# Five stages of an eight-stage fp32 network: order of work in the prologues, one step's maxima, a rotary shuffle and one weight transfer

## The chip, the cores and the metric

The kernel runs on one core of one Trainium2 chip. Time is device microseconds from start to end of the program; the kernel before takes 2041.01 us (median of 3 runs, 2038.54 to 2042.52). Engines are named as in the profile: PE (matrix engine; PEld its weight loads), DVE (vector), ACT (scalar), POOL (GpSimd), SP (issues the DMAs). Each engine runs its own queue of instructions in order and waits on semaphores.

## What is computed

Four pairs of an attention block and a feed-forward block on x of 4 x 512 x 256 values, each with a layer norm ahead and a residual add. The changed stages are the four attentions and the first feed-forward block.

```python
x = x + _L0_attn_ref(_layernorm(x, axis=-1), ...)   # rotary, ALiBi, window mask, 16 heads of 16, 8 kv heads
x = x + _L0_ffn_ref(_layernorm(x, axis=-1), ...)    # silu(x @ Wg.T) * (x @ Wu.T), then @ Wd.T, 256 -> 1024 -> 256
x = x + _L1_attn_ref(_layernorm(x, axis=-1), ...)   # causal, 16 heads of 16
x = x + _L1_ffn_ref(x, ...)                         # spline table
x = x + _L2_attn_ref(_layernorm(x, axis=-1), ...)   # causal, rotary
x = x + _L2_ffn_ref(_layernorm(x, axis=-1), ...)    # 8 experts, top 2
x = x + _L3_attn_ref(_layernorm(x, axis=-1), ...)   # not causal, heads mixed between sequences
x = x + _L3_ffn_ref(_layernorm(x, axis=-1), ...)    # 8 experts, top 2
```

## The kernel before

build() runs the stages one after the other with a barrier of all engines between them. X stays in SBUF as 16 tiles of 128 tokens; a batch b (NB = 4) is 4 tiles, 512 tokens. All orders of work are written out by hand: each stage has one program per engine, and the attention loops take small pieces of the next batch's preparation at the steps that a table `plan` gives. In what follows n is the step within a batch (32 steps of a batch) and N the step over all batches (128).

**Stage a0, attention_window (10 to 407 us of the trace).** The prologue prepares batch 0: DVE normalises (L102), PE turns the tiles (L556) and projects them (L568), DVE multiplies by the rotary tables (rotate, L380 and L383), POOL adds the two products (rotated, L298), ACT rounds to the high part (L467) and POOL takes the low part (lower, L306). SP stores the parts and fetches them back in another layout (L240, L243, L256, L259); these fetches end before the first scores (L592). The masks' constant columns in p are written by POOL in two memsets (L317 and L319), and POOL adds the bias to X (add_bias, L293). Batch 1's statistics are taken in the prologue also; its 1/sqrt is made by POOL (layer_norm_pool, L114 and L116), DVE then applies it (L102) and sums it (total, L343). In the loop DVE takes minima of the scores (L361), ACT the exponentials (L492), PE turns and multiplies them.

**Stage f0, swiglu (407 to 573 us).** SP loads wi (2 MB, L1386) and wd (1 MB, L1387). Weights and inputs are split into a rounded high part (ACT, L1475 and L1478 for weights, L1455 for the input) and a low part (DVE, L1441, L1445 and L1417). PE makes three products for each of KC = 2 chunks of 128 rows (L1503 to L1505), starting with chunk 0. In its queue a wait for all three low weights stands ahead of the loop over batches.

**Stages a1, a2, a3, attention_quads (574 to 882, 996 to 1335, 1550 to 1887 us).** The prologue: layer norm (L102), PE turns (L1178), ACT rounds weights (L1133, L1135) and input (L1138), DVE takes the low parts (L1039, L1044), PE projects (L1189 to L1191). In the loop, each step N has in PE's queue: scores_T(N) (L1234 to L1243), the scores of two tiles 24 tiles ahead (L1214 to L1219), on odd steps values (L1257), then the piece of the plan. DVE takes two maxima (maxima, L987) and then its part of the piece; ACT takes the exponentials (L1160) and its part. The scores use two PSUM banks, so PE waits in scores for the maxima of two tiles back.

The maxima of a group of heads are put together once in 8 steps: POOL's split_maxima (L938, L947, L948) makes two columns of them, PE turns these at n = 6, 14, 22, 30 (turn_maxima, L1265), and ACT and DVE copy them into q (L1095 and L992). POOL runs split_maxima at N % 8 == 4, as the last thing of the step. Its other work in the loop without rotary (a1, a3) is split_kept (L930, L932: two operations) for each turned or projected unit; at n = 12 there is one. With rotary (a2) DVE's rotate (L1012, L1013) ends in a stream_shuffle (L1016) of the sine product, POOL adds the two products (rotated, L907), ACT rounds (upper, L1091) at n = 6, 9, 11, 14 (`raised`) and POOL takes the low part (L914). In a2 the projections stand at n = 4, 7, 9, 12.

Of the kernel before, what the change touches and what calls it, by code (L numbers as in the profile page):

```python
# [13 lines left out]
NB = 4  # L14
S = 512
# [103 lines left out]
def attention_window(nc, tag, X, cst, PS, scr, weights, rope, scale, dist, slopes, bias):  # L119
# [12 lines left out]
    with ExitStack() as ctx:  # L132
# [87 lines left out]
        with nc.Block() as block:  # L220
# [52 lines left out]
            def _(pool):  # L273
# [35 lines left out]
                layer_norm_pool(pool, ln, 0, neg_half)  # L309
                weigh(0)  # L310
                rotated(0, 0)
                lower(0, 0)
                rotated(0, 1)
# [3 lines left out]
                pool.memset(p[:, :, :, KW:S], 0.0).then_inc(tails_done, 1)  # L317
                pool.wait_ge(tails_done, 1)
                pool.memset(p[0:GLOB, :, 0, :], 1.0).then_inc(p_ready, 1)  # L319
                add_bias(0)  # L320
                layer_norm_pool(pool, ln, 1, neg_half)
# [372 lines left out]
def attention_quads(nc, tag, X, Y, cst, PS, scr, filled, weights, masks=None, rope=None, bias=None, scrambled=False):  # L694
# [15 lines left out]
    with ExitStack() as ctx:  # L710
# [59 lines left out]
        else:  # L770
# [4 lines left out]
            for i, n in enumerate((4, 7, 9, 12) if rope is not None else (8, 9, 10, 12)):  # L775
                plan[n] = ("project", 1, i)
        raised = {6: 0, 9: 1, 11: 2, 14: 3} if rope is not None else {}
# [58 lines left out]
        with nc.Block() as block:  # L836
# [56 lines left out]
            def _(pool):  # L893
# [66 lines left out]
                for N in range(FULL):  # L960
                    kind, b, i = piece_at(N)
                    if kind == "turn":
# [9 lines left out]
                    if N % 8 == 4 and N // 8 + 1 < NB * NG:  # L972
                        split_maxima(N // 8 + 1)

            @block.vector
            def _(dve):
# [30 lines left out]
                def rotate(b, u, bank):  # L1007
# [5 lines left out]
                    dve.tensor_tensor(comp[:, u % 2, 0, :], PS[:, bank, :], tabs[:, 0, :], ALU.mult).then_inc(cos_done, 1)  # L1013
                    dve.wait_ge(sin_done, NU * b + u + 1)
# [22 lines left out]
                for i, w in enumerate((wqk_in, wv_in)):  # L1037
# [3 lines left out]
                                      ALU.subtract).then_inc(w_low_done, 1)  # L1041
                for c in range(KC):
                    dve.wait_ge(split_x, c + 1)
                    dve.tensor_tensor(x_low[:, c, :], PS[:, c, :], xnT[:, c, :].bitcast(F32),  # L1044
                                      ALU.subtract).then_inc(x_done, 1)
                if rope is not None:
                    dve.wait_ge(loaded_tab, 16)
                    for u in range(NU):
                        rotate(0, u, (2 + u) % 4)
                else:  # L1050
# [12 lines left out]
                for N in range(FULL):  # L1063
# [3 lines left out]
                    piece(*piece_at(N))  # L1067
                    if N % STEPS == 24 and N // STEPS + 2 < NB:
# [8 lines left out]
            def _(act):  # L1077
# [56 lines left out]
                act.wait_ge(loaded_v, 16)  # L1134
                act.activation(w_high[1][:, :, :].rearrange("p a b -> p (a b)"), wv_in, ACT.Copy).then_inc(w_high_done, 1)  # L1135
                for c in range(KC):
                    act.wait_ge(transposed, c + 1)
                    act.activation(xnT[:, c, :], PS[:, c, :], ACT.Copy).then_inc(split_x, 1)  # L1138
# [214 lines left out]
def swiglu(nc, tag, X, cst, PS, w_in, w_down):  # L1353
# [7 lines left out]
    with ExitStack() as ctx:  # L1361
# [21 lines left out]
        with nc.Block() as block:  # L1383
# [100 lines left out]
            def _(pe):  # L1484
# [8 lines left out]
                def batch(b, ahead):  # L1493
# [13 lines left out]
                    if ahead:  # L1507
                        turn(b + 1)
# [1323 lines left out]
```

## Time and profile before

| | |
|---|---|
| median of 3 runs | 2041.01 us (2038.54 to 2042.52) |
| the profiled execution | 2034.73 us |
| its span, first to last instruction | 2032.8 us |
| PE busy | 1631.1 us, 80% |
| DVE busy | 1186.2 us, 58% |
| ACT busy | 977.1 us, 48% |
| POOL busy | 470.7 us, 23% |
| mean granted PE clock | 0.878 of full speed |

Read it as an average over eight stages, each with limits of its own. A stage begins with a chain of engines that hand one batch to each other, with PE idle most of the time; after that PE is busy nearly always. A clock of 0.5 in a stretch is the 1.2 GHz level, 1.0 the 2.4 GHz level.

### The profile page before, as it was taken

What the parts mean: (1) busy time and instruction counts of PE and PEld (TensorE: products, weight loads), DVE (VectorE), ACT (ScalarE), POOL (GpSimd) and SP (SyncE); (2) the same over time, 40 slices, a digit from 0 to 9 for tenths busy, and PEclk for the clock granted to TensorE, in tenths of its full rate; (3) what the DMA queues carried; (4) which work ended last, traced back from release to release, by engine and by line L of the source; (5) the groups of instructions that cost most, each with busy time, mean ns of one, the idle gap of its engine ahead of it and who ended that gap; (6) DMA issues with size and microseconds to landing.
All of it is one profiled execution on the core that took longest, in us unless ns stands there. A gap on an engine that the chain in (4) does not pass through costs nothing. (4 is left out here: it accounts for less than half of the span.)

```text
span 2032.8 us, 29515 instructions
## 1 busy us (share of the span) xinstructions
PE 1631.1 (80%) x10710; PEld 1004.2 (49%) x10710; DVE 1186.2 (58%) x2606; ACT 977.1 (48%) x1547; POOL 470.7 (23%) x546
## 2 busy tenths in 40 slices
PE   3899999869968999921268899959996799988676
PEld 2455555558855555511245555546775344433433
DVE  2576767442345664659756665545444677775375
ACT  1677879632314544523024444536663366566321
POOL 4220210022323322020222321015664323210100
PEclk8799999979977999965559888978998699899598
DMA  6242240010044345010155325031112355140322
GB/s 212 52 100 53 63 94 1 1 63 0 0 139 120 93 115 146 2 48 0 54 130 146 104 59 130 1 118 47 48 48 70 98 145 142 36 114 1 112 84 84
DMA packets 66900, 156.14 MB, mean 77 GB/s; under 512 B 9853, under 2 KB 15366, under 8 KB 65994
## 3 DMA queue, kind: packets, MB, share of 16 engines
q1 hardware_dynamic: 66762, 154.32, 27.1%
q8 instruction: 84, 1.38, 0.3%
q14 instruction: 54, 0.44, 0.1%
HBM read 104.86 MB, written 51.52 MB: 77 GB/s over the span
## 5 line engine op out<-in xcount | busy, mean ns | idle before, releaser
L987 DVE TENSOR_REDUCE a_mx<-PS 128x1 f32<-128x512 f32 (+3 forms) x768 | 396.0, 553 | 199.8 <-PE PS L1219 124.3
L1160 ACT ACTIVATE a_pT<-PS 128x1024 f32<-128x1024 f32 (+3 forms) x384 | 308.7, 811 | 241.4 <-PE PS L1243 174.6
L1214 PE MATMUL PS<-a_k,a_q 64*128 64x512 f32 (+3 forms) x768 | 251.4, 452 | 68.4 <-DVE a_mx L987 39.0
L361 DVE CUSTOM_DVE_ANT_0 PS<-PS,a_dist 128x448 f32<-128x448 f32 x256 | 155.0, 648 | 72.0 <-PE PS L592 71.0
L1234 PE MATMUL PS<-a_q,a_k 64*128 64x512 f32 (+3 forms) x768 | 180.9, 451 | 11.3 <-DVE a_q L992 6.1
L1214 PEld LDWEIGHTS PS<-a_k,a_q 64*128 64x128 f32 x768 | 117.0, 204 | 128.0 <-DVE a_mx L987 93.2
L1257 PE MATMUL PS<-a_pT,a_va 128*32 128x512 f32 (+3 forms) x1536 | 173.0, 524 | 6.0 <-ACT a_raw L1118 6.0
L492 ACT ACTIVATE a_p<-PS,a_negm 128x448 f32<-128x448 f32 (+1 forms) x256 | 149.2, 640 | 3.4 <-DVE a_negm L361 1.9
L602 PE MATMUL PS<-cst,a_p 128*128 128x128 f32 x1024 | 143.1, 282 | 4.4 <-ACT a_pT L500 1.9
L1234 PEld LDWEIGHTS PS<-a_q,a_k 64*128 64x128 f32 x768 | 80.2, 193 | 117.0 <-issue 90.7
L602 PEld LDWEIGHTS PS<-cst,a_p 128*128 128x128 f32 x1024 | 110.9, 142 | 38.2 <-issue 32.7
L500 ACT ACTIVATE a_pT<-PS 128x512 f32<-128x512 f32 x205 | 115.0, 604 | 28.2 <-PE PS L602 26.8
L1926 POOL TENSOR_TENSOR f_h_low<-f_prod,f_h_high 128x512 fp32r<-128x512 f32 x84 | 109.5, 1310 | 60.9 <-ACT f_h_high L2113 56.0
L1095 ACT ACTIVATE a_q<-PS 16x1024 fp32r<-16x1024 f32 x48 | 48.7, 1016 | 104.1 <-PE PS L1265 103.8
L2049 DVE TENSOR_TENSOR f_prod<-PS,f_gb 128x512 f32<-128x512 f32 x84 | 57.3, 687 | 68.0 <-ACT PS L2139 66.0
L1217 PE MATMUL PS<-a_half_masks 64*128 64x128 bf16 x512 | 92.5, 245 | 0.0
L592 PE MATMUL PS<-a_k,a_q 48*128 48x448 f32 x256 | 63.2, 490 | 26.5 <-ACT a_p L492 16.8
L2139 ACT ACTIVATE PS<-PS,f_b 128x512 f32<-128x512 f32 x84 | 55.5, 660 | 51.1 <-PE PS L2213 51.0
L938 POOL TENSOR_TENSOR a_mxh<-a_mx,a_m 128x16 fp32r<-128x16 f32 x48 | 10.9, 227 | 294.5 <-DVE a_mx L987 294.5
L1219 PE MATMUL PS<-a_half_masks 64*128 64x64 bf16 x512 | 76.3, 201 | 0.0
L592 PEld LDWEIGHTS PS<-a_k,a_q 48*128 48x128 f32 x256 | 25.2, 192 | 100.3 <-issue 57.1
L992 DVE TENSOR_SCALAR a_q<-PS 16x1024 fp32r<-16x1024 f32 x48 | 59.0, 1230 | 20.9 <-PE PS L1265 19.9
(342 smaller groups left out, 3433.3 us busy)
## 6 DMA issues: line engine op xcount, KB each, us to landing
spread_scratch<-a_high SPq DMA_DIRECT2D x96, 256.0 KB, 6.5
a_q<-spread_scratch SPq DMA_DIRECT2D x96, 256.0 KB, 5.8
a_k<-spread_scratch SPq DMA_DIRECT2D x96, 256.0 KB, 6.6
f_gb<-gate_rows SPq DMA_DIRECT2D x68, 256.0 KB, 5.3
spread_scratch<-a_low SPq DMA_DIRECT2D x48, 256.0 KB, 7.4
window_scratch<-a_high SPq DMA_DIRECT2D x24, 256.0 KB, 2.3
a_q<-window_scratch SPq DMA_DIRECT2D x32, 192.0 KB, 5.9
a_k<-window_scratch SPq DMA_DIRECT2D x32, 192.0 KB, 6.3
```

The lines of the kernel that those rows point to most:

```text
L361: dve.tensor_tensor_reduce(PS[:, bank, 0:KW], PS[:, bank, 0:KW], dt_[:, off:off + KW], float(slopes[2 * pair + a]), 3e38, ALU.add, ALU.min ...
L492: act.activation(p[p0:P, GH * (gg % 2) + i, qt, 0:KW], PS[p0:P, bank, 0:KW], ACT.Exp, bias=negm[p0:P, bank:bank + 1], scale=-1.0).then_inc ...
L500: act.activation(pT[:, J % 2, i, :], PS[:, 4 + e % 2, :], ACT.Copy).then_inc(turned_act, 1)
L592: pe.matmul(PS[:, 2 * (N % 2) + a, 0:KW], q[rows, slot, half, qt * P:(qt + 1) * P], k[rows, slot, half, GLOB:S], start=True, stop=True).th ...
L602: mm = pe.transpose(PS[:, 4 + e % 2, qt * P:(qt + 1) * P], p[:, GH * (gg % 2) + i, qt, kt * P:(kt + 1) * P], ident)
L987: dve.tensor_reduce(mx[:, gg % 2, qt, 2 * half + a:2 * half + a + 1], PS[:, 4 + a, 0:kw], AX.X, ALU.max).then_inc(max_done, 1)
L1160: act.activation(pT[:, N // 2 % 2, N % 2, :, q0:S], PS[:, 2 * (N % 2):2 * (N % 2) + 2, q0:S], ACT.Exp, scale=SCALE).then_inc(exp_done, 1)
L1214: mm = pe.matmul(ps[:, 0:kw], q[rows, b % 2, pair, qt * P:(qt + 1) * P], k[rows, b % 2, pair, 0:kw], start=True, stop=not causal)
L1217: pe.matmul(ps[:, kw - P:kw], half_masks[rows, 0, 0, :], half_masks[rows, 1, 0, :], start=False, stop=False)
L1234: mm = pe.matmul(PS[:, 2 * half + a, q0:S], k[rows, b % 2, pair, kt * P:(kt + 1) * P], q[rows, b % 2, pair, q0:S], start=True, stop=not ca ...
L1257: mm = pe.matmul(PS[BLK * i:BLK * i + BLK, 6, q0:S], va[:, b % 2, kt, GH * g + i, :], pT[:, J % 2, i // 2, i % 2, q0:S], start=(kt == 0), ...
L1926: pool.tensor_tensor(h_low[:, G % 6, :], prod[:, G % 6, :], h_high[:, G % 6, :].bitcast(F32), ALU.subtract).then_inc(h_low_done, 1)
```

## The change

In a0, POOL's two memsets of p move: the first behind the first 1/sqrt, the second behind lower(0, 0); the 1/sqrt of batch 1 goes ahead of the bias add of batch 0. In f0, wi comes in two transfers with a semaphore each, ACT and DVE split chunk 0 of the weights, then the input, then chunk 1, and PE waits for chunk 0 before its first product, for chunk 1 before the first product with it, and for the low part of wd ahead of the down projection. In the three quads stages ACT and DVE split the input ahead of the v weights, and split_maxima goes to the head of POOL's step. In a2 the shuffle becomes a function of its own (exchange), which in the loop runs one step after the products (`swaps`); in the prologue it follows them at once, as before.

```diff
@@ attention_window, POOL @@
                 layer_norm_pool(pool, ln, 0, neg_half)
+                pool.memset(p[:, :, :, KW:S], 0.0).then_inc(tails_done, 1)
                 weigh(0)
                 rotated(0, 0)
                 lower(0, 0)
+                pool.wait_ge(tails_done, 1)
+                pool.memset(p[0:GLOB, :, 0, :], 1.0).then_inc(p_ready, 1)
                 rotated(0, 1)
                 lower(0, 1)
                 rotated(0, 2)
                 lower(0, 2)
-                pool.memset(p[:, :, :, KW:S], 0.0).then_inc(tails_done, 1)
-                pool.wait_ge(tails_done, 1)
-                pool.memset(p[0:GLOB, :, 0, :], 1.0).then_inc(p_ready, 1)
+                layer_norm_pool(pool, ln, 1, neg_half)
                 add_bias(0)
-                layer_norm_pool(pool, ln, 1, neg_half)
                 add_bias(1)
@@ attention_quads @@
+        swaps = {5: 0, 8: 1, 10: 2, 13: 3} if rope is not None else {}
         raised = {6: 0, 9: 1, 11: 2, 14: 3} if rope is not None else {}
@@ POOL @@
                     kind, b, i = piece_at(N)
+                    if N % 8 == 4 and N // 8 + 1 < NB * NG:
+                        split_maxima(N // 8 + 1)
                     if kind == "turn":
...
-                    if N % 8 == 4 and N // 8 + 1 < NB * NG:
-                        split_maxima(N // 8 + 1)
@@ DVE @@
+                def exchange(b, u):
                     dve.wait_ge(sin_done, NU * b + u + 1)
                     dve.wait_ge(cos_done, NU * b + u + 1)
                     dve.stream_shuffle(comp[:, u % 2, 1, :], comp[:, u % 2, 1, :], swap).then_inc(swapped, 1)
...
-                for i, w in enumerate((wqk_in, wv_in)):
+                def weights_low(i, w):
...
+                weights_low(0, wqk_in)
                 for c in range(KC):
                     dve.wait_ge(split_x, c + 1)
...
+                weights_low(1, wv_in)
...
                         rotate(0, u, (2 + u) % 4)
+                        exchange(0, u)
...
                     piece(*piece_at(N))
+                    if N % STEPS in swaps and N // STEPS + 1 < NB:
+                        exchange(N // STEPS + 1, swaps[N % STEPS])
@@ ACT @@
-                act.wait_ge(loaded_v, 16)
-                act.activation(w_high[1][:, :, :].rearrange("p a b -> p (a b)"), wv_in, ACT.Copy).then_inc(w_high_done, 1)
                 for c in range(KC):
                     act.wait_ge(transposed, c + 1)
                     act.activation(xnT[:, c, :], PS[:, c, :], ACT.Copy).then_inc(split_x, 1)
+                act.wait_ge(loaded_v, 16)
+                act.activation(w_high[1][:, :, :].rearrange("p a b -> p (a b)"), wv_in, ACT.Copy).then_inc(w_high_done, 1)
@@ swiglu, SP @@
-                sp.dma_start(wi[:, :, :].rearrange("p a b -> p (a b)"), w_in[:, :]).then_inc(loaded_i, 16)
+                for c in range(KC):
+                    sp.dma_start(wi[:, c, :], w_in[:, c * 2 * HID0:(c + 1) * 2 * HID0]).then_inc(loaded_i[c], 16)
@@ DVE @@
+                weights_low(0)
                 input_low(0)
+                weights_low(1)
@@ ACT @@
+                weights_high(0)
                 input_high(0)
+                weights_high(1)
@@ PE @@
                             for c in range(KC):
+                                if n == 0 and part == 0:
+                                    pe.wait_ge(w_low_done, c + 1)
...
+                    pe.wait_ge(w_low_done, KC + 1)
                     for t in range(TB):
...
                 turn(0)
-                pe.wait_ge(w_low_done, KC + 1)
```

POOL's queue in the prologue of a0 (a_p is p, X<-X,a_bb the bias add, a_comp rotated, a_low lower), as one piece of the difference:

```order
 L116 TENSOR_TENSOR a_ln_rstd<-a_ln_vareps,a_neg_half 128x4
+L310 MEMSET a_p 128x32x64
 L284 TENSOR_SCALAR a_ln_xn<-a_ln_xn,a_cplx 128x256 x4
...
-L317 MEMSET a_p 128x32x64
-L319 MEMSET a_p 64x8x512
-L293 TENSOR_TENSOR X<-X,a_bb 128x256 x4
+L315 MEMSET a_p 64x8x512
...
+L114 TENSOR_TENSOR a_ln_vareps<-a_ln_meanvar,a_ln_eps 128x4
+L116 TENSOR_TENSOR a_ln_rstd<-a_ln_vareps,a_neg_half 128x4
+L293 TENSOR_TENSOR X<-X,a_bb 128x256 x8
```

The first memset now follows batch 0's 1/sqrt at once, with no wait ahead of it; the second 1/sqrt has neither memset nor bias add ahead of it, and all eight bias adds follow it.

DVE's queue in a2 at the projection of n = 12 of batch 2 (L987 is a maximum, L1012 and L1013 the two products, L1016 the shuffle, L992 the copy of the maxima). Before:

```order
L987 TENSOR_REDUCE a_mx<-PS 128x1 x2
L1012 TENSOR_TENSOR a_comp<-PS,a_tabs 128x512
L1013 TENSOR_TENSOR a_comp<-PS,a_tabs 128x512
L1016 STREAM_SHUFFLE a_comp<-a_comp 128x512
L987 TENSOR_REDUCE a_mx<-PS 128x1 x4
L992 TENSOR_SCALAR a_q<-PS 16x1024
```

And now:

```order
L988 TENSOR_REDUCE a_mx<-PS 128x1 x2
L1013 TENSOR_TENSOR a_comp<-PS,a_tabs 128x512
L1014 TENSOR_TENSOR a_comp<-PS,a_tabs 128x512
L988 TENSOR_REDUCE a_mx<-PS 128x1 x2
L1020 STREAM_SHUFFLE a_comp<-a_comp 128x512
L988 TENSOR_REDUCE a_mx<-PS 128x1 x2
L993 TENSOR_SCALAR a_q<-PS 16x1024
```

Two maxima, those of the next step, pass the shuffle.

## Rows read from the trace of the kernel before

**Rows 1.** Timeline of a0: start us, duration us, engine, line, operation [idle before <-releaser].

```profile
44.94 0.74 PE L592 MATMUL PS<-a_k,a_q 48*128 48x448 f32 x2 [9.38 <-DMA a_k<-window_scratch]
49.11 1.38 DVE L102 TENSOR_SCALAR a_ln_xn<-X,a_ln_meanvar,a_ln_rstd 128x256 f32<-128x256 f32 x4 [11.04 <-POOL a_ln_rstd L116]
50.64 1.09 PE L556 MATMUL PS<-cst,a_ln_xn 128*128 128x128 f32 x4 [4.96 <-DVE a_ln_xn L102]
53.58 1.21 ACT L492 ACTIVATE a_p<-PS,a_negm 64x448 f32<-64x448 f32 x2 [1.11 <-DVE a_negm L361]
54.81 0.60 ACT L455 ACTIVATE a_xT<-PS 128x512 f32<-128x512 f32 x1
55.55 3.75 PE L568 MATMUL PS<-a_xT,a_wqk 128*128 128x512 f32 x4
```

**Rows 2.** Timeline: the norm alone (a0), beside POOL (f0), beside a memset (f3).

```profile
13.79 1.38 DVE L102 TENSOR_SCALAR a_ln_xn<-X,a_ln_meanvar,a_ln_rstd 128x256 f32<-128x256 f32 x4 [1.50 <-POOL a_ln_rstd L116]
...
439.66 2.37 DVE L102 TENSOR_SCALAR f_ln_xn<-X,f_ln_meanvar,f_ln_rstd 128x256 f32 x4
...
1890.26 1.81 POOL L2363 MEMSET f_wts<- 128x2048 f32 x1
1890.35 2.83 DVE L102 TENSOR_SCALAR f_ln_xn<-Y,f_ln_meanvar,f_ln_rstd 128x256 f32<-128x256 f32 x4 [1.48 <-POOL f_ln_rstd L116]
```

**Rows 3.** DMA issues of f0: engine, KB each, us from issue to landing.

```profile
f_wi<-in_f_in SPq DMA_DIRECT2D x1, 2048.0 KB, 7.6
f_wd<-in_f_down SPq DMA_DIRECT2D x1, 1024.0 KB, 9.7
```

**Rows 4.** Timeline of f0, prologue (L1503 at 426.46 is the first of chunk 1).

```profile
414.87 3.71 ACT L1475 ACTIVATE f_wi_high<-f_wi 128x2048 fp32r<-128x2048 f32 x2 [16.00 <-DMA f_wi<-in_f_in]
416.81 4.50 DVE L1441 TENSOR_TENSOR f_wi_low<-f_wi,f_wi_high 128x2048 fp32r<-128x2048 f32 x2 [4.86 <-ACT f_wi_high L1475]
421.23 1.28 DVE L1417 TENSOR_TENSOR f_x_low<-PS,f_x_high 128x512 fp32r<-128x512 f32 x2
425.05 0.76 PE L1503 MATMUL PS<-f_x_high,f_wi_high 128*128 128x512 f32 x1 [11.06 <-DVE f_wd_low L1445]
426.46 0.63 PE L1503 MATMUL PS<-f_x_high,f_wi_high 128*128 128x512 f32 x1
```

**Rows 5.** Waits of PE in a1 (590 to 900 us): total us, times, longest.

```profile
PE PS L1265 <- POOL a_m L948: 4.3, 3, 1.4
```

**Rows 6.** Waits of PE in a3 (1550 to 1886 us).

```profile
PE PS L1265 <- POOL a_m L948: 4.5, 3, 1.6
```

**Rows 7.** Timeline of a1 and a3 at n = 12 to 14 of batch 0.

```profile
654.24 1.23 DVE L992 TENSOR_SCALAR a_q<-PS 16x1024 fp32r<-16x1024 f32 x1 [1.48 <-PE PS L1265]
...
1636.37 1.23 DVE L992 TENSOR_SCALAR a_q<-PS 16x1024 fp32r<-16x1024 f32 x1 [1.17 <-PE PS L1265]
```

**Rows 8.** Timeline of a2, prologue.

```profile
1002.94 0.63 ACT L1135 ACTIVATE a_w_highv<-a_pT 128x512 fp32r<-128x512 f32 x1 [0.98 <-DMA a_pT<-in_a_w]
1004.21 1.28 DVE L1044 TENSOR_TENSOR a_x_low<-PS,a_xnT 128x512 fp32r<-128x512 f32 x2
```

**Rows 9.** Waits of PE in the loop of a2 (1060 to 1238 us).

```profile
PE PS L1214 <- DVE a_mx L987: 13.6, 16, 1.4
PE PS L1265 <- POOL a_m L948: 2.3, 6, 0.4
```

**Rows 10.** Timeline of a2 from n = 4 to 9 of batch 0.

```profile
1061.71 0.73 DVE L1016 STREAM_SHUFFLE a_comp<-a_comp 128x512 f32<-128x512 f32 x1
1074.32 0.63 ACT L1091 ACTIVATE a_high<-a_comp 128x512 fp32r<-128x512 f32 x1 [0.95 <-POOL a_comp L907]
```

**Rows 11.** Windows in a1 and a2: us, PE, PEld, DVE, ACT, POOL busy, PEclk, DMA, GB/s.

```profile
716.61:733.72 17.11, 16.35 (x161) 10.10 (x161) 9.45 (x19) 7.94 (x12) 0.63 (x3) 1.00 0.82 224
782.63:802.14 19.51, 18.87 (x161) 11.61 (x161) 9.37 (x19) 8.00 (x12) 0.63 (x3) 0.83 0.88 227
1055.00:1245.00 190.00, 168.41 (x1518) 101.17 (x1519) 120.32 (x262) 83.02 (x123) 52.19 (x69) 0.88 0.39 106
```

More of the change, by code:

```diff
@@ L1374, in swiglu @@
         h_high, h_low = sb("h_high", [P, NHT, S], R32), sb("h_low", [P, NHT, S], R32)
-        loaded_i, loaded_d, preset = sem("loaded_i"), sem("loaded_d"), sem("preset")
+        loaded_i = [sem(f"loaded_i{c}") for c in range(KC)]
+        loaded_d, preset = sem("loaded_d"), sem("preset")
         w_high_done, w_low_done = sem("w_high_done"), sem("w_low_done")
@@ L1438, in _, with weights_low @@
                 layer_norm_dve(dve, ln, 0, lambda t: X[:, t, :])
-                for c in range(KC):
+                def weights_low(c):
                     dve.wait_ge(w_high_done, c + 1)
@@ L1471, in batch, with weights_high @@
                         input_high(b + 1)
-                act.wait_ge(loaded_i, 16)
-                for c in range(KC):
+                def weights_high(c):
+                    act.wait_ge(loaded_i[c], 16)
                     act.activation(wi_high[:, c, :], wi[:, c, :], ACT.Copy).then_inc(w_high_done, 1)
+                weights_high(0)
                 input_high(0)
+                weights_high(1)
                 act.wait_ge(loaded_d, 16)
```

## The prediction

> **What bounds the kernel now.** The page's busy shares come first: PE 80%, DVE 58%, ACT 48%, POOL 23%. PE bounds the sum, so a change pays where it ends idle time of PE or raises PE's clock (mean 0.878). The timeline of each prologue comes next, since PE idles there for long, then the waits of PE within each loop, and at last windows with the clock beside them. The reader is to see in each who comes last.
>
> In a0 PE's first scores wait for the DMA that brings the keys back and start at 44.94 [rows 1]. Batch 1 is not ready then: DVE has stood for 11.04 us, since 38.07, for POOL's 1/sqrt, and normalises only at 49.11; PE turns the tiles at 50.64, projects at 55.55 [rows 1]. In f0 PE's first product waits for the low part of wd, the last thing DVE does, and starts at 425.05 [rows 4]. In a1 and a3 PE stands for POOL's maxima, 4.3 and 4.5 us, three times each [rows 5, 6]. In a2 PE waits for DVE's maxima, 13.6 us in 16 waits, 0.85 each [rows 9].
>
> **a0.** Without the memsets and the bias add ahead of it, POOL makes batch 1's 1/sqrt soon after its last lower, some 3 us after DVE's statistics (38.07), near 41. DVE's norm takes 1.38 and is done before the scores start at 44.94, so the fetches bound the chain. From there, with the row's durations: the scores' 0.74 to 45.7, PE's turn 1.09, ACT's copy 0.60, the first exponential 1.21, the second copy 0.60, and about 0.1 between each: the projection starts at 49.6 instead of 55.55, a gain of 5.95 [rows 1]. If the chain from turn to projection kept its present length (50.64 to 55.55) behind a turn at 45.75, it would be 4.9.
>
> What it costs: the first memset now runs right behind batch 0's 1/sqrt, at the time DVE normalises batch 0, which is on the chain that ends in the fetches. Alone this norm takes 1.38; beside a memset of the same size in f3 it takes 2.83 [rows 2]. So +1.45 on everything behind. The bias add may now run beside batch 1's norm: beside one POOL operation it took 2.37, 1.0 more [rows 2]; but the scores still start later than that norm ends, so I take 0.3 (0 to 1.0). The second memset fits into POOL's idle time between the units of the prologue. Net 5.95 − 1.45 − 0.3 = **−4.2** (−2.5 to −6.0).
>
> The Trainium skill, "SBUF — State Buffer", section "Who interferes with whom", says of DVE in a two-port mode and GpSimd that "Whoever issues first gets the shared pair for the whole instruction; the other fully blocks". By that the norm waits for the whole memset, 1.8 instead of 1.45; the row of f3 shows the collision and 1.45, some less than the rule, so the trace agrees in kind.
>
> **f0.** wi lands 7.6 after its issue (at 414.8), wd 9.7 (417.3) [rows 3]: the second MB takes about 2.5 longer per MB, so the first half of wi should land at 412.3. ACT's copy of a chunk is 3.71/2 = 1.87, DVE's low part 4.50/2 = 2.25, the input's low part 1.28 [rows 4]. ACT has chunk 0 at 414.3; DVE is at it until 416.6 and has the input at 417.9; PE starts at 418.0 instead of 425.05. DVE's chunk 1 is done at 420.2, and PE's first product with it starts at 420.3 instead of 426.46: **−6.1**. The clock's rise moves with it. wd's low part follows 2.3 later, long before the down projection. If both halves land together at 414.8, each step is 2.3 later: −3.8.
>
> **a1, a3.** split_maxima goes ahead of split_kept in POOL's queue at n = 12. PE's turn then has its operand in time, and the next to be late would be DVE: in a1 it stood 1.48 behind that turn, in a3 1.17 [rows 7], so it gives nearly the whole wait back. split_kept comes some 0.7 later, for a projection a step away. **−4.2** and **−3.0**. ACT's and DVE's turned order in the prologue: the v weights are there before the input in a1 (0); in a3 −0.3 (0 to −0.6).
>
> **a2.** In the prologue ACT waits 0.98 for the v weights, and only then DVE takes x's low part, for which PE waits [rows 8]; now the input goes first: **−1.0**. In the loop DVE's shuffle, 0.73 [rows 10], no longer stands between the products and the next step's two maxima. The same shuffle then stands after the next step's maxima, where DVE has waits of its own (it does 120 us of work in 190 [rows 11]). PE's waits for the maxima and for POOL's turns are 13.6 + 2.3 = 15.9 [rows 9]; that is the upper bound. Against it: the two products alone take 1.4 and remain, and the parts come later: POOL adds the products after the shuffle, and ACT, which already waits 0.95 for that sum at n = 9 [rows 10], would wait some 2.3 longer, with the next exponentials behind it. I take 0.6 of 15.9, **−9.5** (−4 to −15.9).
>
> **Clock.** Equal work (161 matmuls) in a1 takes 17.11 at 1.00 and 19.51 at 0.83, 2.40 more [rows 11]. At half speed for 0.34 of 19.51 the records lose the equivalent of 3.3 full-speed us, so each costs 0.73. The loop of a2 stands at 0.88 for 190 us [rows 11]: 22.8 such us, worth 16.6. With fewer waits of PE part of it returns; I take a fifth, **−3** (0 to −15). That is my least certain term.
>
> The Trainium skill, "TensorE: Matmul & The Clock Gate", section "Terms", puts the penalty at the throttled time × (1 − K/N), which would make the dip of a1 3.3 and a2's 22.8; the trace has 2.40 for the first, so the sum goes by 0.73.
>
> **The sum.** 4.2 + 6.1 + 4.2 + 3.3 + 1.0 + 9.5 = 28.3, and 3 of clock: 31.3. The profiled execution took 2034.73 (span 2032.8), so 2003.4 for one like it. The median of the runs is 2041.01, 6.3 above that execution: 2009.7, or **2010**.
>
> **Rivals.**
> - *The clock returns in full.* If PE without gaps keeps the full clock in most of a2's loop and the dips of a1 and a3 go, the clock's term is −18 instead of −3: 1995. For it: the dip in a1 [rows 11]. Against: a2's 0.88 is a mean over 190 us, and PE still waits for ACT and DVE.
> - *The loops pay little.* Another engine takes each wait over: in a2 ACT at its wait for the sum, in a1 and a3 DVE at the copy of the maxima. Then the prologues' 11.6 remain, and some 2 to 3: 2027. For it: DVE is the busier one in a2, the maxima at a projection keep 1.4 of products ahead of them.
> - *Slower.* In a2 the shuffle a step later makes the sum 2.2 to 2.6 later; ACT's queue is in order, so at each of 12 projections the exponentials behind its copy are late, and PE stands for them. It decides if ACT has under 1 us of slack at each; at 2.6 × 12 = 31 lost, with a2's 9.5 and the clock's 3 not gained, the sum is 31 − 18.8: +12, 2053. Against: ACT is busy 83 of 190 us and PE waits for an exponential nearly nowhere.
> - *The change doesn't do what it says*: the memset holds DVE longer in a0, both halves of wi land together, and the waits in the loops remain with another name: 2038.
>
> **How the numbers follow.** Forecast 0.60, full clock 0.13, loops pay little 0.18, slower 0.04, no effect 0.05. The forecast's own bounds are a2 at −4, no clock and wi together (8 more, with a0 at its low end 10 more: 2020) and a2's 15.9 with some more clock (10 less: 2000). The range reaches on to the first two rivals, 1995 to 2027, and leaves out the last two and half of the first, with what lies beyond either end. A measurement of this kernel can tell 0.2%, 4.1 us, from no change: faster 0.91 (the first three cases), same 0.05, slower 0.04.
>
> **What the profile of the changed kernel would show.** Right: in a0 the norm of batch 0 at about 2.8 and no 11 us wait ahead of batch 1's, scores at about 46.4, the projection near 51.3. In f0 wi in two rows, the first landing about 5 after its issue and PE's first product 11 after it (18 before). In a1 and a3 no wait of PE for POOL at the turn. In a2 the waits for DVE's maxima at half or less, longer waits of ACT for POOL's sum. Wrong: these waits gone and PE waiting for ACT in their place; a norm of batch 0 at 1.4 (my cost is not there) or over 3; a clock in a2 that stays at 0.88 or reaches 0.95.

## Result and profile after

The changed kernel takes 1986.79 us (median of 4 runs, 1979.97 to 1990.48) against 2040.71 before: ratio 0.9732, 95% interval 0.9704 to 0.9761, or 54 us less. Timed once more on another chip it took 1985.39 against 2034.42: ratio 0.9767, 0.9738 to 0.9796, 49 us less. The profiled execution took 1990.48, its span is 1988.6, 44.2 less than the span of before.

From one stage's first norm to the next one's, in us, by the two traces:

| | a0 | f0 | a1 + f1 | a2 | f2 | a3 | f3 |
|---|---|---|---|---|---|---|---|
| before | 396.8 | 166.6 | 422.3 | 340.0 | 213.6 | 337.3 | 142.5 |
| changed | 392.7 | 160.6 | 414.9 | 320.0 | 214.4 | 329.2 | 142.9 |
| difference | −4.1 | −6.1 | −7.4 | −20.0 | +0.8 | −8.1 | +0.4 |

The two stages that the change doesn't touch stay within 0.8. a0 and f0 paid what the prediction gave them; the three stages with the quads loop paid far more.

The page, engines' busy time and the granted clock in 40 slices:

```profile
PE 1618.9 (81%) x10710; PEld 999.2 (50%) x10710; DVE 1183.9 (60%) x2606; ACT 977.4 (49%) x1547; POOL 472.3 (24%) x546
PEclk9899999979977999965569999869998799999598
```

PE executes the same 10710 instructions as before, yet its busy time is 12 us less: its instructions ran faster.

Timeline of a0 (start us, duration us, engine, line), the answer to [rows 1, 2]:

```profile
13.85 1.80 POOL L310 MEMSET a_p<- 128x2048 f32 x1
13.93 2.83 DVE L102 TENSOR_SCALAR a_ln_xn<-X,a_ln_meanvar,a_ln_rstd 128x256 f32<-128x256 f32 x4 [1.50 <-POOL a_ln_rstd L116]
L102 DVE TENSOR_SCALAR a_ln_xn<-X,a_ln_meanvar,a_ln_rstd x4: 394/401/1864, 13.9 to 16.4; 128x256 f32<-128x256 f32 x4
42.12 2.92 DVE L102 TENSOR_SCALAR a_ln_xn<-X,a_ln_meanvar,a_ln_rstd 128x256 f32<-128x256 f32 x4 [3.01 <-POOL a_ln_rstd L116]
46.01 0.74 PE L592 MATMUL PS<-a_k,a_q 48*128 48x448 f32 x2 [9.41 <-DMA a_k<-window_scratch]
50.43 3.75 PE L568 MATMUL PS<-a_xT,a_wqk 128*128 128x512 f32 x4
```

The norm of batch 0 takes 2.83 beside the memset, the figure taken from f3. The third line has the shortest, the median and the longest of its four instructions in ns: one is held and takes 1.86 us, until 15.79, just behind the memset's end at 15.65; the others take 0.40 as without a memset. The wait of 11.04 is 3.01, the scores start 1.07 later than before, the projection of batch 1 5.12 earlier.

DMA issues and timeline of f0's prologue, the answer to [rows 3, 4] (the stage's first norm stands at 406.67 here, at 410.58 before):

```profile
f_wi<-in_f_in SPq DMA_DIRECT2D x2, 1024.0 KB, 6.0
```

```profile
408.33 1.91 ACT L1492 ACTIVATE f_wi_high<-f_wi 128x2048 fp32r<-128x2048 f32 x1 [15.50 <-DMA f_wi<-in_f_in]
410.28 2.29 DVE L1455 TENSOR_TENSOR f_wi_low<-f_wi,f_wi_high 128x2048 fp32r<-128x2048 f32 x1 [2.22 <-ACT f_wi_high L1492]
413.87 0.76 PE L1525 MATMUL PS<-f_x_high,f_wi_high 128*128 128x512 f32 x1 [3.79 <-DVE f_x_low L1430]
416.02 0.79 PE L1525 MATMUL PS<-f_x_high,f_wi_high 128*128 128x512 f32 x1 [0.53 <-DVE f_wi_low L1455]
```

ACT starts 1.66 after the norm's start instead of 4.29, so the first half of wi is there 2.6 earlier, against the norm's start, than the whole was. PE's first product stands at +7.2 instead of +14.5, the first with chunk 1 at +9.35 instead of +15.88: 6.5 earlier.

Waits of PE (total us, times, longest) in a1 (580 to 883 us), then in a2's loop (1041 to 1206), then in a3 (1553 to 1841), the answer to [rows 5, 6, 9]; of each the first line:

```profile
PE PS L1225 <- DVE a_mx L988: 8.3, 15, 0.9
...
PE PS L1225 <- DVE a_mx L988: 5.2, 10, 0.6
...
PE PS L1225 <- DVE a_mx L988: 10.6, 18, 1.1
```

No wait for POOL at the turn (it would be L1276) is left anywhere, and none took its place: in a1 the wait for maxima is 8.3 where it was 8.4 before. In a2 the 15.9 of [rows 9] are 5.2. Behind the first scores, to the stage's end, the same two waits are 18.1 before (15.8 and 2.3) and 7.4 now: 10.7 less either way.

Windows of a2's loop (us, PE, PEld, DVE, ACT, POOL busy, PEclk, DMA, GB/s), the answer to the last of [rows 11]:

```profile
1041.00:1211.00 170.00, 157.39 (x1552) 96.59 (x1553) 121.54 (x270) 84.18 (x125) 49.07 (x66) 0.98 0.44 119
```

1552 matmuls in 170 us, where 1518 took 190, and the clock is 0.98 instead of 0.88. The two places in this loop where it still falls to the 1.2 GHz level, at 1106 and 1174, stand right behind its two longest waits, 1.65 us each for POOL's low part of x (L1200, at 1104.7 and 1173.0); none stands behind a wait for maxima, of which the longest is 0.6:

```profile
1104.00:1112.00 8.00, 7.29 (x62) 4.31 (x62) 5.38 (x10) 2.12 (x4) 2.42 (x5) 0.79 0.01 2
```

ACT's timeline in a2 shows what the late shuffle costs:

```profile
1053.70 0.63 ACT L1102 ACTIVATE a_high<-a_comp 128x512 fp32r<-128x512 f32 x1 [1.52 <-POOL a_comp L908]
```

ACT waits 1.52 where it waited 0.95 [rows 10], 8.3 instead of 5.2 in 190 us of the loop, and PE waits for no exponential behind it.

### The profile page after: what moved, and what is told of

Its sections match the earlier page's. It is cut to its first block and busy times, and to the rows that moved or that the text cites. A ratio compares the mean times of both kernels' runs of the same rounds, so it can differ in the third digit from the quotient of the medians.

```text
span 1988.6 us, 29520 instructions
## 1 busy us (share of the span) xinstructions
PE 1618.9 (81%) x10710; PEld 999.2 (50%) x10710; DVE 1183.9 (60%) x2606; ACT 977.4 (49%) x1547; POOL 472.3 (24%) x546
## 3 DMA queue, kind: packets, MB, share of 16 engines
q8 instruction: 84, 1.38, 0.3%
## 5 line engine op out<-in xcount | busy, mean ns | idle before, releaser
L616 PE MATMUL PS<-a_pT,a_va 128*32 128x512 f32 x512 | 68.8, 611 | 0.0
```

## Experiments

What was open: which part brought how much, and whether the excess over the prediction is the clock, a part that was priced too low, or a difference between runs. Runs of one kernel differ by up to 25 us on one chip (the kernel before: 2022.77 to 2047.90 in 27 runs, with the clock from 0.869 to 0.885), so each run is read by its ratio and by its stages. The ratios come from different chips, and each has its interval.

| | median | before, same chip | ratio (95%) | a0 | f0 | a1 + f1 | a2 | a3 | f3 |
|---|---|---|---|---|---|---|---|---|---|
| a0_pool | 2030.65 | 2035.81 | 0.9997 (0.9971–1.0023) | 389.3 | 166.7 | 428.5 | 337.1 | 336.8 | 142.4 |
| f0_split | 2030.74 | 2035.81 | 0.9982 (0.9950–1.0013) | 398.1 | 162.4 | 423.2 | 337.3 | 336.8 | 142.7 |
| maxima_first | 2017.65 | 2035.81 | 0.9927 (0.9898–0.9955) | 398.1 | 167.1 | 415.4 | 336.9 | 326.9 | 142.5 |
| shuffle_lag | 2030.93 | 2035.81 | 0.9981 (0.9954–1.0007) | 397.9 | 167.1 | 421.1 | 340.5 | 332.4 | 141.4 |
| pair | 1997.62 | 2039.01 | 0.9807 (0.9765–0.9850) | 397.6 | 167.0 | 415.1 | 316.3 | 327.5 | 141.8 |
| no_lag | 2003.72 | 2039.01 | 0.9838 (0.9792–0.9884) | 394.3 | 160.6 | 415.0 | 339.6 | 325.6 | 139.3 |
| dose | 1988.86 | 2039.01 | 0.9750 (0.9707–0.9794) | 393.8 | 161.9 | 416.1 | 327.2 | 332.4 | 139.9 |
| dose_long | 1994.57 | 2035.49 | 0.9802 (0.9760–0.9844) | 391.6 | 160.6 | 417.7 | 327.8 | 326.4 | 142.7 |
| memsets_behind | 1980.65 | 2039.01 | 0.9726 (0.9684–0.9768) | 392.7 | 160.6 | 415.2 | 316.3 | 327.4 | 138.7 |
| spread | 1985.17 | 2035.49 | 0.9758 (0.9723–0.9794) | 392.5 | 160.6 | 415.2 | 316.9 | 327.2 | 139.2 |
| combined | 1984.20 | 2035.49 | 0.9751 (0.9722–0.9780) | 390.3 | 160.4 | 415.0 | 319.9 | 326.8 | 138.2 |
| changed_again | 1985.39 | 2034.42 | 0.9767 (0.9738–0.9796) | 390.5 | 161.4 | 416.6 | 315.8 | 329.3 | 139.7 |
| memsets_again | 1983.01 | 2034.42 | 0.9746 (0.9715–0.9776) | 392.7 | 160.7 | 415.1 | 316.2 | 329.8 | 139.2 |

The stages are of one profiled execution each. Traces with the same code for a stage lie up to about 4 us apart in a0, a2 and f3 and up to 7 in a1 + f1 and a3, so a single difference of that size tells nothing.

### The parts one at a time

**a0_pool**: POOL's queue of a0 as in the diff of the change, all else as before.

> The kernel before with a0's order on POOL alone. Theory (each part is worth its own stall): norm of batch 0 at 2.8 us beside the memset, the 11 us wait of batch 1's norm gone, stage a0 4.0 shorter, run 4 us faster, the clock of the other stages as before. Rival (the clock of later stages hangs on when they start, so any shift changes it): stage a0 4.0 shorter, but stages a1 to a3 differ from the kernel before by more than 3 us.

a0 is 389.3 here, 7.5 less than before in one trace each; f0, a3 and f3 stay within 0.5, a1 + f1 is 6.2 longer and a2 2.9 shorter. By the letter this is what the rival expected, but a1 + f1 has 421 to 428 in the four kernels whose code of it is the same, and a2 337 to 340 in three, so differences of this size come without any change to POOL in a0. Whether the start time plays a part is not shown. The run's ratio tells nothing at this size: the interval holds both 0 and 4 us. The gain is better read from PE's projection in the trace of the changed kernel, 5.1 earlier, and from a0 in all traces: 392.1 on the mean of the seven with this order, 397.7 of the five with the old one, 5.6 less.

**f0_split**: f0 as in the diff of the change, all else as before.

> The kernel before with the changed f0 alone (two transfers of wi, chunk order on ACT, DVE and PE). Theory: f0 6.1 shorter, PE's first product 7.2 after the first norm instead of 14.5, run 6 us faster, the other stages the same within 2 us. Rival: as f0, with a1 to a3 moved by over 3 us in either direction.

f0 is 162.4 where the kernels with the old order have 166.6 to 167.1, and 160.4 to 161.9 in those with the whole change: 4 to 5 gained here, 6 there. The median is 5.1 lower, and the interval of the ratio holds that and nothing as well. a1 + f1 is within 1 of the kernel before, a2 2.7 shorter and a3 0.5; none of this is over 3, so the rival finds nothing for it.

**maxima_first**:

```diff
                     kind, b, i = piece_at(N)
+                    if N % 8 == 4 and N // 8 + 1 < NB * NG:
+                        split_maxima(N // 8 + 1)
                     if kind == "turn":
...
-                    if N % 8 == 4 and N // 8 + 1 < NB * NG:
-                        split_maxima(N // 8 + 1)
```

> The kernel before with split_maxima at the head of POOL's step alone, in a1, a2 and a3. Theory (a clock dip follows PE's wait for POOL and goes with it): PE's waits at the turn 4.3, 2.3 and 4.5 us go, and the dips at n = 14 of a1 and a3 with them, 3 to 5 us more; run 12 to 16 us faster, a1 6 and a3 7.5 shorter. Rival (the clock is not tied to these waits): 9 to 11 us faster, the dips of a1 and a3 at the same places.

18 us by the medians, about 15 by the ratio. a1 + f1 is 415.4; the eleven traces with this order of POOL have 414.9 to 417.7, the four without it 421.1 to 428.5: on the mean 8.2 apart, for a wait of 4.3. a3 has 325.6 to 332.4 with it and 332.4 to 337.3 without it, 7.8 apart on the mean, for a wait of 4.5. So each us of such a wait that goes takes nearly one more with it.

The theory tied this to dips of the clock, the stretches at the 1.2 GHz level. The loop of a1, up to its last batch, before and with split_maxima first:

```profile
631.00:866.00 235.00, 218.30 (x2206) 133.56 (x2206) 138.38 (x299) 119.98 (x178) 51.79 (x78) 0.98 0.36 95
633.00:868.00 235.00, 220.17 (x2268) 134.63 (x2266) 140.08 (x303) 122.72 (x184) 51.72 (x78) 1.00 0.36 95
```

In the kernel before, PE waits 1.4 us for POOL at 653.6, 716.6 and 782.6, and the clock falls at 654.5 and 784.2, not behind the second. In the four traces with these waits a dip begins within 3 us of 8 of the 12, and nowhere else in this stretch; in the eleven without them ten have no dip and one has one, at another place (dose, 850). So in a1 the wait brings the dip, though not each time, and this may be a part of what differs between runs of one kernel. In a3 it is less plain: the dips of the kernel before stand at 1620 and 1733, its waits for POOL at 1635.7, 1703.9 and 1781.4, and most traces without these waits keep one or two dips.

But a2 gives nothing (336.9 against 337.1 to 340.0), though the wait for POOL is gone there as well. The waits of PE in 190 us of its loop say why:

```profile
PE PS L1214 <- DVE a_mx L987: 14.8, 16, 1.4
```

The wait for DVE's maxima grew from 13.6 to 14.8 [rows 9]: what one wait gave, the other took for the most part. The clock of this loop stays at 0.88, with eleven dips, each behind a wait of 0.86 or more.

**shuffle_lag**: exchange as a function of its own and one step later in a2's loop, as in the diff of the change, all else as before.

> The kernel before with the shuffle one step behind its products in a2's loop, nothing else. Theory (PE's waits at projections bring the dips): PE's waits for maxima in a2's loop fall from 13.6 to about 5, the granted clock of that loop rises from 0.88 to 0.95 or more, a2 is 14 to 19 us shorter and the run as much faster, ACT's waits for the sum 2 us longer without any wait of PE for ACT. Rival 1 (only the waits count): a2 8 to 9 shorter with the clock at 0.88. Rival 2 (the sum comes too late): PE waits for ACT's exponentials, a2 less than 6 shorter.

a2 is 340.5, no shorter than before, and neither the theory nor its two rivals had the reason. The waits of PE in 190 us of the loop, then POOL (its sum and the last operation of split_maxima) and PE at n = 4 to 6:

```profile
PE PS L1272 <- POOL a_m L949: 13.2, 6, 2.2
PE PS L1221 <- DVE a_mx L988: 5.0, 10, 0.5
```

```profile
1064.08 1.26 POOL L908 TENSOR_TENSOR a_comp<-a_comp 128x512 f32<-128x512 f32 x1 [5.53 <-DVE a_comp L1020]
1065.77 0.23 POOL L949 TENSOR_TENSOR a_m<-a_mx,a_mxh 128x16 f32<-128x16 f32 x1
```

```profile
1066.14 1.09 PE L1272 MATMUL PS<-cst,a_m 128*128 128x128 f32 x4 [2.19 <-POOL a_m L949]
```

The wait for maxima fell to 5.0 as expected. But POOL's queue is in order: it stands at n = 4 for the shuffle, which now comes a step later, and split_maxima is behind its sum. PE's turn waits 2.2 for it at each of 6 places, 13.2 instead of the 2.3 of [rows 9]. The gain of one queue was handed to another.

### Together

**pair**: the kernel before with both of the last two.

> The kernel before with the two changes of the attention loops together: split_maxima at the head of POOL's step, and the shuffle one step behind. Theory now (the two only pay together in a2: with the shuffle late, POOL's sum stands ahead of split_maxima and PE's turn waits 13.2 us for it; with split_maxima early alone, PE waits 14.8 for DVE): a2's loop has neither wait, maxima at about 6, a2 16 to 20 us shorter, a1 6 and a3 8 to 10 shorter; run 34 to 42 us faster, more than the 18 and 5 of the two apart. Rival (the parts add up): 20 to 26 us faster, a2 3 shorter.

41 us faster, as the theory had it and 15 more than its rival's upper end; a2 is 316.3, 23.7 less than in the kernel before, where 16 to 20 was expected. Of a2 this gives a square:

| a2, us | shuffle at once | shuffle a step later |
|---|---|---|
| split_maxima last | 337.1 to 340.0 (3 traces) | 340.5 |
| split_maxima first | 336.9, 339.6 | 315.8 to 320.0 (5 traces of 3 kernels) |

Either alone is worth nothing in a2, both are worth 20 us. PE's waits in its loop:

```profile
PE PS L1221 <- DVE a_mx L988: 5.8, 11, 0.6
```

**no_lag**: the changed kernel with the shuffle put back.

```diff
                     elif kind == "project" and rope is not None:
                         rotate(b, i, 7)
+                        exchange(b, i)
...
                     piece(*piece_at(N))
-                    if N % STEPS in swaps and N // STEPS + 1 < NB:
-                        exchange(N // STEPS + 1, swaps[N % STEPS])
```

> The changed kernel with the shuffle back behind its products at once. Theory (the two only pay together): PE's waits for maxima in a2's loop back at 14 to 15, clock of a2 0.86, a2 16 to 20 longer, run 16 to 22 slower than the changed kernel, 32 to 38 faster than the kernel before. Rival (the lag is worth only what it was alone): run 5 or less slower than the changed kernel, about 50 faster than before.

17 us above the changed kernel's median, or 14 to 22 by the ratios (0.9838 against 0.9767 and 0.9732), a2 339.6, and the wait for maxima is back (14 to 15 expected):

```profile
PE PS L1224 <- DVE a_mx L988: 12.9, 15, 1.4
```

This shows from the other side that a2 needs the lag as well. What the rest of the change brings is the difference of pair and the changed kernel: 1997.62 to 1986.79, 10.8 us (8 to 15 by the ratios, on different chips), of which a0 has 4.9 and f0 6.4 by the stages (397.6 and 167.0 against 392.7 and 160.6). The reordered weights of the quads stages had no run of their own. PE's wait for x's low part in the prologue went from 2.7 to 1.6 in a2 and from 3.4 to 2.7 in a3, and stayed at 1.5 in a1; the times can't tell a gain of this size.

### Waits and clock

**dose** and **dose_long**: the changed kernel with one DVE instruction more at each of the 12 projections of a2's loop; its result is not used.

```diff
                     elif kind == "project" and rope is not None:
                         rotate(b, i, 7)
+                        dve.tensor_reduce(ln.held[:, 1:2], tabs[:, 0, 0:256], AX.X, ALU.max)
```

> The changed kernel with one more DVE instruction behind the two products at each projection of a2's loop, a maximum over 128x256 of the rotary table into an unused column, about 0.35 us, 12 times. Theory (the clock falls where PE's waits at the projections grow): PE waits some 0.3 longer at each, 3 to 4 us in all, and the dips of a2 come back in part: a2 5 to 9 us longer, clock of its loop 0.92 to 0.95. Rival (the clock is not tied to these waits): a2 4 or less longer and its clock as in the changed kernel.

> The changed kernel with the extra maximum of each projection over 128x512 instead of 128x256, about 0.6 us instead of 0.4. Theory (the clock falls where PE's waits at the projections grow, and the dose before was too small to tell in the runs' times): PE's waits for maxima in a2's loop at 13 or more, the loop's clock at 0.90 or less, a2 12 or more longer than the changed kernel's, run 10 to 18 slower than it. Rival (the clock is not tied to the waits): a2 and run 5 to 8 slower, the waits alone, with the loop's clock as it was.

The waits for maxima in 190 us of the loop were 6.3 in 12 in the changed kernel, and of the two doses:

```profile
PE PS L1226 <- DVE a_mx L988: 9.9, 17, 0.9
```

```profile
PE PS L1226 <- DVE a_mx L988: 12.6, 17, 1.1
```

They grew by 3.6 and 6.3, where 3 to 4 was expected of the first and 13 or more in all of the second. The windows of 190 us of the loop, dose, then dose_long, then no_lag:

```profile
1040.40:1230.40 190.00, 173.59 (x1668) 106.24 (x1665) 131.07 (x293) 89.41 (x133) 52.48 (x72) 0.95 0.45 117
```

```profile
1038.70:1228.70 190.00, 171.03 (x1623) 104.00 (x1621) 131.27 (x288) 86.92 (x131) 52.78 (x72) 0.94 0.41 110
```

```profile
1038.80:1228.80 190.00, 171.73 (x1532) 102.55 (x1528) 120.82 (x263) 82.76 (x124) 51.73 (x69) 0.86 0.38 103
```

With these kernels side by side, PE's waits for maxima (and for POOL at the turn) in such 190 us, the longest of them, the loop's clock and the stage. The two waits of 1.6 for POOL's low part, which every one of them has, are left out:

| | waits, us | longest | clock | a2, us |
|---|---|---|---|---|
| before | 13.6 + 2.3 | 1.4 | 0.88 | 340.0 |
| shuffle_lag | 5.0 + 13.2 | 2.2 | 0.88 | 340.5 |
| maxima_first | 14.8 | 1.4 | 0.88 | 336.9 |
| no_lag | 12.9 | 1.4 | 0.86 | 339.6 |
| dose_long | 12.6 | 1.1 | 0.94 | 327.8 |
| dose | 9.9 | 0.9 | 0.95 | 327.2 |
| changed | 6.3 | 0.6 | 0.97 | 320.0 |
| pair | 5.8 | 0.6 | 0.98 | 316.3 |

The clock falls as the waits grow, so it is tied to them, as the theory had it for the first dose (0.92 to 0.95 expected, 0.95 found; its a2 is 7 to 11 longer than the two traces of the changed kernel, 320.0 and 315.8, for 3.6 us of waits). But their sum is not the measure: dose_long and no_lag have nearly the same sum, 0.94 against 0.86, and 12 us between them. Nor does each dip stand behind one of the lengthened waits: the two of dose begin at 1116.0 and 1204.7, 2.5 to 2.7 us behind waits of 0.36, and none follows its waits of 0.8 at once. One thing that differs between dose_long and no_lag is the length of the single wait, 1.1 against 1.4 at the longest; no run separates it from the places where the waits stand. Of dose_long a clock of 0.90 or less was expected, and a2 12 or more longer: the clock came out at 0.94 and a2 8 to 12 longer. That figure for the clock falls. The run's time does not decide: 10 to 18 slower was expected, and it is 7.8 by the medians, 7 to 14 by the ratios (0.9802 against 0.9767 and 0.9732). How much of the clock one wait of a given length costs stays open.

### POOL beside DVE

**memsets_behind** and, with another chip, **memsets_again**:

```diff
                 layer_norm_pool(pool, ln, 0, neg_half)
+                pool.wait_ge(ln.xn_done, TB)
                 pool.memset(p[:, :, :, KW:S], 0.0).then_inc(tails_done, 1)
...
                 layer_norm_pool(pool, ln, 1, neg_half)
+                pool.wait_ge(ln.xn_done, 2 * TB)
                 add_bias(0)
...
                 layer_norm_pool(pool, ln, 0, neg_half)
-                pool.memset(wts[:, :, :], 0.0).then_inc(preset, 1)
-                for b in range(1, NB):
+                layer_norm_pool(pool, ln, 1, neg_half)
+                pool.wait_ge(ln.xn_done, 2 * TB)
+                pool.memset(wts[:, :, :], 0.0).then_inc(preset, 1)
+                for b in range(2, NB):
```

> The changed kernel with POOL's first memset of a0 behind the norm of batch 0, the bias add behind the norm of batch 1, and f3's memset behind the norm of its batch 1. Theory (DVE's norm shares something with POOL's memset and bias add): the three norms at 1.38 instead of 2.83, 2.92 and 2.83; a0 1.5 to 2 shorter, f3 1.4 shorter, run 3 us faster than the changed kernel. Rival (the norm of batch 0 is not on the chain that ends in the fetches): norms at 1.38, a0 the same within 0.3.

> The version with POOL's memsets and bias add behind the norms, beside the changed kernel on one chip. Theory (norms at 1.38 pay in a0 and f3): 1.5 to 5 faster than the changed kernel. Rival (the fetches of a0 and the tail of f3 take the gain): within 1.5 of it.

All three norms take 1.38 again, those of a0 and that of f3. f3 has 138.7 and 139.2 with it, against 142.9 and 139.7 of the changed kernel, which tells nothing. In a0 PE's products show where the gain goes. The changed kernel first, then memsets_behind:

```profile
19.56 5.64 PE L568 MATMUL PS<-a_xT,a_wqk 128*128 128x512 f32 x8 [0.78 <-ACT a_xT L455]
```

```profile
18.06 6.28 PE L570 MATMUL PS<-a_xT,a_wqk 128*128 128x512 f32 x8 [0.78 <-ACT a_xT L457]
45.33 0.74 PE L594 MATMUL PS<-a_k,a_q 48*128 48x448 f32 x2 [9.59 <-DMA a_k<-window_scratch]
```

The first eight products start 1.50 earlier and take 6.28 instead of 5.64, so the next ones (at 25.04 and 24.18) are only 0.86 earlier, and the scores 0.68 (0.29 in the pair of traces of the other chip, 45.40 and 45.11). a0 as a whole is 392.7 in both, so of 1.45 on the norm 0.3 to 0.7 was left at the scores and nothing can be seen at the stage's end. The medians are 6.1 below the changed kernel's and, side by side on one chip, 2.4 (ratios 0.9746 and 0.9767, whose intervals overlap). It is not shown to be faster.

**spread**: the changed kernel with smaller DVE pieces in the three loops. **combined**: this with the memsets moved.

```diff
                 def exchange(b, u, bank):
+                    dve.tensor_tensor(comp[:, u % 2, 0, :], PS[:, bank, :], tabs[:, 0, :], ALU.mult).then_inc(cos_done, 1)
...
-                    if N % STEPS == 24 and N // STEPS + 2 < NB:
-                        layer_norm_stats(dve, ln, N // STEPS + 2, source(N // STEPS + 2))
...
+                        if N % STEPS == 23:
+                            for t in range(TB // 2):
+                                dve.bn_stats(ln.stats[:, t, :], source(c)(t)).then_inc(ln.stats_done, 1)
+                        if N % STEPS == 24:
+                            layer_norm_stats(dve, ln, c, source(c), TB // 2)
+                        if N % STEPS == 26:
+                            dve.wait_ge(transposed, KC * c)
+                            layer_norm_apply(dve, ln, c, source(c), 0, TB // 2)
+                        if N % STEPS == 28:
+                            layer_norm_apply(dve, ln, c, source(c), TB // 2)
```

> The changed kernel with the DVE pieces of the three attention loops cut smaller: the cosine product one step behind the sine product, with the shuffle; the statistics of the norm over two steps (23 and 24), its application over two (26 and 28). Theory (what is left of PE's waits for maxima hangs on how much DVE does between them): waits for maxima in a2's loop from 6.3 to about 3, a2 3 to 6 shorter, a1 and a3 about 1 each; run 4 to 8 faster than the changed kernel. Rival (the cosine product late frees PE's bank late, or the step after has the longer piece now): no gain.

> The two versions together: POOL's memsets and bias add behind the norms, and the smaller DVE pieces. Theory: 8 to 14 us faster than the changed kernel, 1972 to 1979. Rival (the smaller pieces gain nothing): as the version with the memsets moved alone, 1981.

No gain that can be told: 1985.17 and 1984.20. In a2's loop the waits of spread are:

```profile
PE PS L1232 <- DVE a_mx L988: 5.0, 12, 0.6
PE PS L1275 <- ACT a_raw L1136: 2.9, 7, 0.6
```

What DVE gave (6.3 to about 5), ACT took: the wait for a_raw, ACT's copy of the finished values, went from about 1 to 2.9. This is neither of the rival's two reasons.

## Why the prediction was wrong

The direction and the terms of the prologues were right; the time lies 8 us below the range. 1986.8 was measured where 2010 was forecast with 1995 as the low end.

- **a0**: −4.2 forecast, −4.1 in the stage (−4.9 of pair against the changed kernel). The norm beside the memset came out at 2.83 to the hundredth. The bias add cost batch 1's norm 1.5 instead of 1.0 (2.92), without delaying the scores, which was the argument. But the cost of the first collision, charged at its full 1.45, is 0.3 to 0.7 at the scores by the runs with the memset moved. By the Trainium skill, "SBUF — State Buffer", section "Who interferes with whom", the later one "fully blocks". The page says this of a two-port mode of DVE, and no run shows which mode this norm is in; but the trace agrees: its first instruction is held until just behind the memset's end, and the norm ends at 16.76, where 1.38 from the memset's end (15.65) would give 17.03.
- **f0**: −6.1 forecast, −6.1 in the stage. The first half of wi came 2.6 earlier (2.5 forecast), chunk 1's product 6.5 earlier.
- **a1 and a3**: waits of 4.3 and 4.5 gone (4.2 and 3.3 taken), nothing in their place. The stages gave 7.4 and 8.1.
- **a2**: prologue as forecast (−1.1). The loop's waits went from 15.9 to 5.2, 10.7 where 9.5 was taken. The reason given for taking only 0.6 of them did not come true: ACT was to wait 2.3 longer for the sum, with the exponentials behind it, and waited 0.6 longer, with PE waiting for none. The sum was right in part by luck of grouping: 13.6 and 2.3 were added as waits of two edits, each worth its own, when the runs show that each is worth nothing without the other. A third rival, a wait that jumps between POOL and DVE when only one is removed, was missing; it did not decide since the change has both.
- **Clock**: this is the step that failed. "With fewer waits of PE part of it returns; I take a fifth, −3". By the stages less the waits it returned 3.1 in a1 (7.4 − 4.3), 3.6 in a3 (8.1 − 4.5) and 8.2 in a2 (20.0 − 10.7 − 1.1), 14.9 together. Added up over the dips in the traces, the full-speed time lost fell from 86.5 to 81.2 in a1 and f1, from 48.8 to 37.1 in a2 and from 35.5 to 29.8 in a3: 22.7, at 0.73 each 16.6. The granted clock of a2's loop rose to 0.98, and the prediction itself had named 0.95 there as a sign of being wrong. Nothing in the profile spoke for a fifth: in a1 and in a2's loop nearly all dips of the kernel before stood right behind waits that were to go, though not in a3. The first rival ("the clock returns in full", −18) had the mechanism and the size nearly right, with a chance of 0.13 that was too low. The term's own bounds (0 to −15) just hold the 14.9, but the range of the sum did not carry them along. That waits and dips go together is shown by maxima_first in a1 and by pair and no_lag in a2; the doses show it by degrees in the mean clock, not dip by dip.
- **The price of clock**: 0.73 us for each full-speed us lost. For a2 it gives (48.8 − 37.1) × 0.73 = 8.5, measured 8.2. The Trainium skill, "TensorE: Matmul & The Clock Gate", section "Terms", counts the full share, 11.7, so the traces do not agree with it here. The runs of the kernel before say the same: over the 56 of them on three chips, a straight line through time against lost time (the span times what its mean clock lacks of 1) rises 0.70 us for each us lost.
- **From one execution to the median**: "6.3 above that execution" was carried over to the changed kernel. Its profiled execution is instead 3.7 above its median. This is 10 of the 23 us by which the forecast missed. It is not a thing apart from the clock: that execution has 0.886, the other three 0.891 to 0.895. Where both kernels ran on one chip, the median clock went from 0.877 to 0.8905 and the lost time from 250 to 217, which at 0.70 is some 23 us of the 49 (an estimate). So between medians the clock's term is still further from 3 than the 15 of the two traces. The range held nothing for this.

Counted up: 31.3 forecast; +11.9 clock; +1.3 in a2 (10.7 + 1.1 against 9.5 + 1.0); +1.3 in a1 and a3, where the whole waits of 4.3 and 4.5 went and 4.2 and 3.3 were taken; −1.2 in the stages not touched: 44.6, against 44.2 in the traces. The clock's 14.9 is what the stages' waits leave over, so this sum must nearly close; the dips are the measure that does not hang on it. The choice of executions adds 10: 54.

## To carry to other kernels

Where a step of one queue is late for two reasons on two engines, ask of each edit alone which wait ends last after it: the two edits here were worth 0 and 0 in a2, and 20 us together. Look at the granted clock beside the waits: where it dips at the very steps whose waits an edit removes, charge those dips to the edit, here some 15 us on top of 20 us of waits in the two traces. A wait of the same length does not dip the clock each time (8 of 12 in a1), so one trace shows a sample. And compare runs, not one execution: add the spread of a kernel's own runs to the range.

## What was not expected of the hardware

- The kernel before alone ranged over 2022.77 to 2047.90 in 27 runs on one chip, with clocks of 0.869 to 0.885: faster runs tend to have the higher clock (2045.78 at 0.870, 2026.92 at 0.885).
- PE's first products after an idle stretch took longer when they started earlier: eight of a0 took 6.28 from 18.06, and 5.64 from 19.56. In both traces a single one takes 1.06 us or more at first and 0.59 from some point between 23.1 and 23.8 us on: begun at 19.56, five of the eight come before it, begun at 18.06, six. The work that is pulled forward runs at the slow rate, so 1.50 earlier at their start is 0.86 at their end.
- DVE's norm beside POOL's bias add, both reading and writing SBUF, took 2.92 instead of 1.38, as much as beside a memset (2.83), but in another way: beside the memset its first instruction took 1.86 us and the other three 0.40; beside four bias adds each of the four took 0.74 to 0.81, and each began 0.10 to 0.14 behind one bias add.
